# Linear attention: one reciprocal over eight heads' denominators instead of one per head

## What is computed

```python
q = second_taylor_expansion(q * dh ** (-0.5))      # 1, q, q*q/sqrt(2): 273 features of 16
k = second_taylor_expansion(k)
kv_state = jnp.einsum('bhnd,bhne->bhde', k, v)
k_sum = jnp.sum(k, axis=2)
den = jnp.einsum('bhnd,bhd->bhn', q, k_sum)
qk_inv = 1.0 / jnp.maximum(den, 1e-5)
out = jnp.einsum('bhnd,bhde->bhne', q, kv_state) * qk_inv[..., None]
out = out.transpose(0, 2, 1, 3).reshape(b, n, h * dh)
return out @ w_out
```

## Time and profile before

| | us |
|---|---|
| timed runs | 8221.56 and 8782.80, median 8502.18 |
| profiled execution | 8223.99 |
| its span on the slowest core (core 3) | 8222.2 |
| spans of the 8 cores | 8170.9 to 8222.2 |
| TensorE, VectorE, ScalarE, GpSimd busy | 6061.9, 2477.3, 1743.1, 152.3 |

### The profile page before, as it was taken

How to read it: one execution, slowest core, us unless ns; L and a number is a source line. 1 busy time by engine, 2 the same in 40 slices (tenths; PEclk the granted TensorE clock), 3 DMA queues, 4 the chain that set the end, 5 groups by cost and what they waited for, 6 DMA issues and landing times.

```text
span 8222.2 us, 72417 instructions; the slowest of 8 cores (8170.9 to 8222.2 us)
## 1 busy us (share of the span) xinstructions
PE 6061.9 (74%) x25424; PEld 2492.6 (30%) x25424; DVE 2477.3 (30%) x5029; ACT 1743.1 (21%) x2768; POOL 152.3 (2%) x177
## 2 busy tenths in 40 slices
PE   3344699999997887787886777936655666676687
PEld 2111244444443333333333333412211121221233
DVE  4645322222222222222223222245443432223000
ACT  1000111111111111111111111110033546474121
POOL 0000000000000000000000000000000000000000
PEclk9555699999998898899998888969876777777898
DMA  1000232233233212212213211110112020201423
GB/s 50 4 0 0 46 62 39 55 62 62 57 82 57 44 36 48 60 31 39 47 29 72 49 39 39 21 55 12 21 35 31 1 31 1 31 1 16 119 73 81
DMA packets 164142, 336.73 MB, mean 41 GB/s; under 512 B 12131, under 2 KB 53900, under 8 KB 161364
## 3 DMA queue, kind: packets, MB, share of 16 engines
q0 software_dynamic: 107888, 221.31, 15.5%
q1 hardware_dynamic: 55908, 110.79, 4.3%
HBM read 445.96 MB, written 46.14 MB: 60 GB/s over the span
## 4 chain that ended last, share of the span: by engine, by line
PE 65%; DVE 10%; DMA 10%; ACT 6%; issue 6%; DVEq 2%; POOL 0%; ACTq 0%; SPq 0%; POOLq 0%
PE pA L701 21%; PE pB L717 11%; PE pC L717 11%; ACT expT L1072 4%; PE pA L1191 3%; DMA denM<-den_stg 2%; DMA wbuf<-L_W 2%; DMA w1t_sc<-buf 2%; PE pB L1205 1%; PE pA L924 1%; PE pC L1205 1%; PE pD L616 1%; DVE recS L586 1%; PE pC L1094 1%; PE pA L1063 1%
## 5 line engine op out<-in xcount | busy, mean ns | idle before, releaser
L701 PE MATMUL pA<-xnT,W1q 128*128 128x512 bf16 x8192 | 1822.7, 384 | 0.0
L706 ACT ACTIVATE h<-pA,b1c 128x512 bf16<-128x512 f32 x1024 | 705.8, 689 | 3711.2 <-PE pA L701 3711.2
L701 PEld LDWEIGHTS pA<-xnT,W1q 128*128 128x128 bf16 x8192 | 808.6, 99 | 988.1 <-issue 50.2
L731 DVE SCALAR_TENSOR_TENSOR acc<-pB,G,acc 128x512 f32<-128x512 f32 x512 | 383.4, 751 | 2241.0 <-PE pB L717 1641.8
L717 PE MATMUL pB<-W2q,h 128*128 128x512 bf16 x4096 | 936.8, 379 | 125.5 <-ACT h L706 120.3
L717 PE MATMUL pC<-W2q,h 128*128 128x512 bf16 x4096 | 937.6, 379 | 0.0
L717 PEld LDWEIGHTS pB<-W2q,h 128*128 128x128 bf16 x4096 | 383.4, 97 | 638.4 <-issue 208.3
L1072 ACT ACTIVATE expT<-pA,shcol 128x512 bf16<-128x512 f32 (+1 forms) x704 | 466.1, 745 | 412.9 <-PE pA L1063 359.5
L731 DVE SCALAR_TENSOR_TENSOR acc<-pC,G,acc 128x512 f32<-128x512 f32 x512 | 383.8, 751 | 537.7 <-PE pC L717 349.8
L717 PEld LDWEIGHTS pC<-W2q,h 128*128 128x128 bf16 x4096 | 390.3, 98 | 482.1 <-issue 29.0
L1079 DVE TENSOR_TENSOR expT<-expT,s_masks 128x512 bf16<-128x512 bf16 (+1 forms) x640 | 270.9, 425 | 808.9 <-ACT expT L1072 793.5
(11 more groups left out here) (252 smaller groups left out, 3777.9 us busy)
## 6 DMA issues: line engine op xcount, KB each, us to landing
W1q<-L_W POOLq DMA_DIRECT2D x32, 2048.0 KB, 18.8
W2q<-L_W POOLq DMA_DIRECT2D x32, 2048.0 KB, 32.4
wbuf<-L_W SPq DMA_DIRECT2D x32, 1024.0 KB, 11.8
w2tb<-w2t_sc POOLq DMA_DIRECT2D x8, 4096.0 KB, 17.1
wbuf<-L_W SPq DMA_DIRECT2D x32, 512.0 KB, 10.6
wbuf<-L_W SPq DMA_DIRECT2D x64, 256.0 KB, 5.0
WOb<-L_WO POOLq DMA_DIRECT2D x8, 2048.0 KB, 15.7
o<-stg POOLq DMA_DIRECT2D x64, 256.0 KB, 4.2
```

Source lines behind the costliest of these rows:

```text
L701: t_p1 = mm.mark(TE.raw.matmul(PS[bk], lhsT=W1q[:, s, a, ft * 128:(ft + 1) * 128], rhs=xnT[:, a, tq * 512:(tq + 1) * 512], start=(a == 0), ...
L706: bank_free[bk] = sc.mark(SE.raw.activation(h1[:, ft, :], PS[bk], ACT.Relu, bias=b1c0[:, e, qq * 8 + ft:qq * 8 + ft + 1]))
L731: bank_free[bk] = vv.mark(VE.raw.scalar_tensor_tensor(out=aslc, in0=PS[bk], scalar=G[:, tq * 4 + ts_, e:e + 1], in1=aslc, op0=OP.mult, op1 ...
```

## The change

The loop over heads is split in two. In the first, ScalarE copies row 0 to a slot of `recS` (`h % 2`), and SyncE moves it to row `h` of a new tile `denL` (8 x 512, f32). Then VectorE clamps all eight rows, takes one reciprocal, and casts it to `recLb` (bf16). In the second, TensorE picks a head's row and broadcasts it to 17 partitions by a bf16 matmul with a slice of a new constant `sel8`, and VectorE multiplies. ScalarE's copy waits for the transfer that last used the slot. `G`, the experts' gates, is no longer allocated ahead of everything, but in `l0_ffn`, and `sel8` is loaded third in SyncE's queue, ahead of `x`. The debugging exits `l0sub` 50 to 52 go.

```diff
+    sel8 = np.zeros((8, 136), dtype=np.float32)
+    for h in range(8):
+        sel8[h, h * 17:(h + 1) * 17] = 1.0
+    c["sel8"] = sel8.astype(bfdt)
...
-    G = es.enter_context(nc.sbuf_tensor("G", [128, NT, 8], F32))
...
+                        denL = sbl(st, "denL", (8, 512), F32)
+                        recLb = sbl(st, "recLb", (8, 512), BF16)
...
-                                SE.wait(t3)
+                                SE.wait(t3, t_dstg2[h % 2])
                                 t_outS = sc.mark(SE.raw.copy(outS[:, h, :], ps17))
-                                t_den = sc.mark(SE.raw.copy(recS[0:1, 0, :], ps17[0:1, :]))
+                                t_den = sc.mark(SE.raw.copy(recS[0:1, h % 2, :],
+                                                            ps17[0:1, :]))
                                 bank_free[bko] = t_den
-                                VE.wait(t_den)
-                                VE.raw.drain()
-                                VE.raw.tensor_scalar(out=recS[0:1, 0, :],
-                                                     in0=recS[0:1, 0, :],
-                                                     scalar1=1e-5, scalar2=None, op0=OP.max)
-                                VE.raw.drain()
-                                t_rec = vv.mark(VE.raw.reciprocal(recS[0:1, 1, :],
-                                                                  recS[0:1, 0, :]))
+                                t_dd = dma(SY, sd, denL[h:h + 1, :],
+                                           recS[0:1, h % 2, :], deps=(t_den,))
+                                t_dstg2[h % 2] = t_dd
+                                t_dens.append(t_dd)
+                            VE.wait(*t_dens)
+                            VE.raw.drain()
+                            VE.raw.tensor_scalar(out=denL[:], in0=denL[:],
+                                                 scalar1=1e-5, scalar2=None, op0=OP.max)
+                            VE.raw.drain()
+                            VE.raw.reciprocal(denL[:], denL[:])
+                            VE.raw.drain()
+                            t_rcb = vv.mark(VE.raw.tensor_copy(recLb[:], denL[:]))
+                            t_outS_all = sc.tok()
+                            for h in range(8):
                                 bk4 = 4 + h % 2
                                 use_bank(bk4)
-                                TE.wait(t_rec)
-                                mmb = mm.mark(TE.raw.matmul(PS[bk4][0:17, :],
-                                                            lhsT=ones_row_f32[0:1, 0:17],
-                                                            rhs=recS[0:1, 1, :],
-                                                            start=True, stop=True))
-                                VE.wait(mmb, t_outS)
+                                TE.wait(t_rcb, tk["consts"])
+                                mmb = mm.mark(TE.raw.matmul(
+                                    PS[bk4][0:17, :],
+                                    lhsT=consts["sel8"][:, h * 17:(h + 1) * 17],
+                                    rhs=recLb[:], start=True, stop=True))
+                                VE.wait(mmb, t_outS_all)
...
+                    G = sbl(st, "G", (128, NT, 8), F32)
```

More of the change, by code:

```diff
@@ L59 @@
 CSHAPES = dict(ident32=(128, 128, F32), ident16=(128, 128, BF16),
+               sel8=(8, 136, BF16),
                ones_row_bf=(1, 128, BF16), ones_row_f32=(1, 128, F32),
@@ L523, in l0_attn @@
                                     allow_slow_non_contiguous=True)
+                        t_dstg2 = [None, None]
                         for cch in range(NCH):
                             t_qf2T = []
+                            t_dens = []
                             t_qf2_used = mm.tok()
@@ L588, in l0_attn @@
-                                if l0sub == 51:
-                                    t_sc_h.append(t_rec)
-                                    continue
+                                t_den = sc.mark(SE.raw.copy(recS[0:1, h % 2, :],
+                                                            ps17[0:1, :]))
+                                bank_free[bko] = t_den
+                                t_dd = dma(SY, sd, denL[h:h + 1, :],
+                                           recS[0:1, h % 2, :], deps=(t_den,))
@@ L607, in l0_attn @@
                                 t_sc_h.append(t_sch)
-                            if l0sub < 6 or l0sub in (50, 51, 52):
+                            if l0sub < 6:
                                 continue
```

## The result

| | before | changed |
|---|---|---|
| timed runs, median us | 8572.93 (10 runs, 8220.90 to 9026.56) | 8630.66 (11 runs, 8126.93 to 9031.94) |
| profiled execution, us | 8223.99 | 8147.95 |
| span, mean of the 8 cores | 8194.9 | 8114.6 |
| ratio of undisturbed runs | | 0.9887, 95% interval 0.9867 to 0.9906 |

The kernel is 1.1% faster, which is within 2%. The others took 8220.90, 8221.56 and 8238.20 us before, and 8126.93, 8132.17, 8135.98 and 8140.07 now, and the ratio is of these.

What follows compares the result with a forecast made beforehand. The experts' matmuls lead the kernel's chain; the changed loop is a chain of waits. Per chunk 69.6 - 48.3 = 21.3 us, 85.2 for four, net 84.7 after one issue: 8139 from 8223.99, range 8085 to 8190.

Steps and rivals of the forecast that it cites:

- the sentence on the two timed runs: Timed runs of 8221.56 and 8782.80 us: the profiled execution, 8223.99, stands with the lower, and so does the forecast 8139.
- Size of the gain: Loop over heads, four chunks: 21.3 us saved per chunk, 85.2 in all, net 84.7 after one added issue.
- First half: First loop over heads, per chunk: matmuls, copies and an exposed transfer hop of 1.86 us per head, 36.8 us for eight.
- The reading of the token rule: Waits on SyncE's semaphore sd are raised to its latest count, so TensorE and ScalarE wait for the previous head's transfer.
- Second half: From clamp to wout matmul, per chunk: 5.27 us to the first product, 5.3 for seven steps, 0.93 after the last.
- The seven steps: Product to product in the second loop: two banks alternate, 1.53 us per two heads, 5.3 in all.
- One issue at the start: SyncE's queue at kernel start: sel8's load ahead of x costs one more issue, 0.43 us, on the path.
- The hidden hop: Rival, first loop: TensorE and ScalarE wait only for the transfer of two heads ago; 87 us more gain, 8052; chance 0.03.
- Quicker stores: Rival, FFN: w1t_sc and w2t_sc stores from buf1's new start move a fifth faster; 59 us, 8080; chance 0.06.
- slower wbuf loads: Rival, FFN: loads to wbuf's new address move at half speed; 164 us more, 8303; chance 0.02.
- The longer hop: Rival, first loop: 4.5 us per hop takes the whole gain, 5.5 us gives 8255; chance 0.03.
- the change would do nothing: Rival, loop over heads: the part stays near 69 us because reciprocals are off the path; chance 0.01.

Runs made afterwards that it cites:

- e1: The changed kernel with a semaphore per staging slot for the den transfers; undisturbed timed runs 8049.68 and 8068.84 us, stage 381.5 us against 467.1.
- e2: The changed kernel with one semaphore of their own for all den transfers; stage 416.8 us against 467.1, mean span 8061.2 us.
- e8: The changed kernel with a bf16 matmul gathering den rows instead of copy and transfer, and second-half broadcasts over four banks; ratio to the kernel before 0.977.
- e3: The kernel before with only G moved into l0_ffn and sel8 added and loaded; undisturbed dies' mean span 8199.6 us against 8198.9, no ratio taken.

## Why the prediction was right in its steps and wrong in its time

**The number.** Forecast 8139 us, range 8085 to 8190; the median is 8630.66, outside. The step that failed is the sentence on the two timed runs, that "the profiled execution stands with the lower one, and so does my figure". That fixed the level of the forecast, and it was left there as if the next median had to stand low as well. Two runs 560 us apart already showed that a median could fall on either side, and no case for it was priced. In its place the runs showed seven of eleven from 8520.49 to 9031.94 us, so that the median fell among these, 58 us above that of the kernel before. Why a die's clock falls in one execution and not in the next stays open; no run here tried it. The four undisturbed runs, 8126.93 to 8140.07, lie at the forecast, and so does the ratio: 8139 / 8223.99 is 0.9897, inside 0.9867 to 0.9906.

**Size of the gain.** Forecast 84.7 us, measured 86.2 in the stage and 80.3 in the mean span. Within 2%, as forecast.

**First half.** 36.8 forecast for eight heads, 435.78 - 399.23 = 36.55 measured. The hop taken from layer 1's attention, 1.86, came out as 1.79 to 1.91 from another engine to another engine. The reading of the token rule, and not the code's two slots, was what fixed this term; e1 and e2 show it by taking it away.

**Second half.** Clamp to first product 5.27 forecast, 441.10 - 435.78 = 5.32 measured. The seven steps: 5.3 forecast; measured, pairs start every 1.51 us and the two of a pair 0.60 apart, 5.13 in all. With VectorE alone it was to be 5.0, and e8 shows 4.2 (0.60 us a product, not 0.71). The mechanism, two banks in turn, was right (1.51 a pair against 1.53); the size taken for VectorE alone, from products on 64 rows, was too large for 17 rows; whether the rows make the difference is not shown. Last product to L620: 0.93 both times.

**One issue at the start.** 0.43 us were forecast for sel8's load. The first kvA matmul comes at 395.9 us before and at 395.4 now, the cores differing among themselves by 6 to 7 us, so this is too small to be seen.

**Page against row.** The Trainium skill (DMA: Bandwidth & Descriptors, section on the anatomy of one DMA) gives its fixed 2.0 us for transfers that GpSimd issues. Those of this loop are issued by SyncE, and in the steady loop a hop with both semaphores is 1.77 to 1.91 us, so the prediction did well to go by the row. Not every hop is that short: of e1's 32 transfers the longest took 3.4 us to land on core 0, where the median is 1.6, and it stands ahead of the third head's copy shown above; the cause was not tried. By the Trainium skill's section on how a descriptor splits into AXI transactions, on the same page, a row is read in fewer beats from buf1's new start; e3 shows no trace of that in the stores' waits, 320.9 us against 321.4.

**Rivals.** The hidden hop did not happen in the changed kernel, and its price came out: 87 us more were forecast for it, e1 brought 85.6. The price was in part luck, since it was worked out from copies and a hop, and e1's pace is set by the matmuls. Quicker stores and slower wbuf loads are refuted by e3. The longer hop did not come. That the change would do nothing is refuted by the stage, 86.2 us shorter.

## What to carry to other kernels

A second buffer overlaps nothing if the token that guards it counts everything on its queue. Before a transfer is put on a semaphore that other engines wait for, list those waits: here a token for loads long done turned into a wait for the last transfer, and with the same wait on ScalarE it cost as much as the change brought. The rule of the token need not go for that: e1 keeps it and gives each slot a semaphore. Where a loop in which no engine is full gets a small transfer, price the whole hop per turn first, and hide it; a matmul that moves the row instead gained no more in this stage. And where timed runs of one kernel lie 560 us apart, forecast the ratio, and give the median a case for each level.

## What was not expected

A second hop that follows the first at once adds 1.70 us, where one hop takes 1.79 to 1.91. Products on 17 rows start every 0.60 us when nothing holds them, though each is recorded with 0.68; those on 64 rows in layer 1's attention start every 0.71. One reciprocal of 512 columns takes 3.34 us on 1, 8 and 32 rows alike, which is why gathering the rows pays.
